# A four-layer transformer kernel: one layer's second residual goes from VectorE to GpSimd, and that layer's loop is written out

## The reference, cut to what matters

```
h   = gamma * norm(x)  + beta
x1  = attention(h) + bp + x              # first residual
out = gamma * norm(x1) + beta + x1       # second residual
```

## Time and profile before

| | |
|---|---|
| median of 3 runs | 1201.8 us (1199.96 to 1210.7) |
| profiled execution | 1202.65 us |
| its span | 1200.8 us |
| TensorE busy in the span | 92% |
| VectorE busy | 67% |
| ScalarE busy | 47% |
| GpSimd busy | 14% |

### The profile page before, as it was taken

The page is one execution under the profiler, slowest core; times in us unless marked ns, Lnnn a source line. Parts: engine busy times, 40 slices in busy tenths (PEclk is TensorE's granted clock), DMA queues, the critical chain, the costliest instruction groups (busy, mean ns, idle before and its releaser), DMA issues.

```text
span 1200.8 us, 22222 instructions
## 1 busy us (share of the span) xinstructions
PE 1100.7 (92%) x7540; PEld 840.9 (70%) x7540; DVE 806.5 (67%) x2245; ACT 560.7 (47%) x1122; POOL 173.5 (14%) x288
## 2 busy tenths in 40 slices
PE   5799999999999999999999988888888999999996
PEld 4567777777777777777777665555555777777765
DVE  4576667666677667766577677777778666776642
ACT  4235554545643455444554434444444455554451
POOL 3010110101102211010110011111114101111010
PEclk9789999999999999999999999999999999999998
DMA  7542333123343233312333323333353133322300
GB/s 234 181 147 72 107 108 92 59 63 105 107 151 147 78 107 107 90 56 70 106 108 116 109 63 115 105 114 112 113 164 124 58 107 116 116 76 65 92 24 18
DMA packets 102714, 123.18 MB, mean 103 GB/s; under 512 B 8992, under 2 KB 96032, under 8 KB 101600
## 3 DMA queue, kind: packets, MB, share of 16 engines
q1 hardware_dynamic: 102048, 121.73, 32.6%
q10 hardware_dynamic: 576, 0.30, 0.1%
HBM read 85.16 MB, written 35.78 MB: 101 GB/s over the span
## 4 chain that ended last, share of the span: by engine, by line
PE 68%; DVE 13%; issue 6%; DMA 5%; ACT 4%; SPq 1%; ACTq 1%; DVEq 0%; POOL 0%; POOLq 0%
PE dense L1160 12%; PE dense L1091 9%; PE s_bank L1184 9%; PE o_bank L1239 8%; PE dense L1146 8%; PE st_bank L1221 6%; DMA q_stack<-max_t 4%; DVE neg_max L790 4%; PE o_bank L1120 3%; PE o_bank L1106 2%; PE o_bank L1070 2%; PE o_bank L1246 2%; PE s_bank L1194 2%; ACT xn L550 2%; DVE s_bank L785 1%
## 5 line engine op out<-in xcount | busy, mean ns | idle before, releaser
L602 ACT ACTIVATE probs<-st_bank 128x512 f32<-128x512 f32 (+1 forms) x512 | 263.8, 568 | 251.8 <-PE st_bank L1221 188.8
L790 DVE TENSOR_REDUCE neg_max<-s_bank 128x2 f32<-128x512 f32 x384 | 256.3, 684 | 70.0 <-PE s_bank L1184 66.1
L1184 PE MATMUL s_bank<-k_stack,q_stack 96*128 96x256 f32 (+1 forms) x1024 | 232.1, 318 | 18.8 <-DMA k_stack<-qk_dram 8.3
L1184 PEld LDWEIGHTS s_bank<-k_stack,q_stack 96*128 96x128 f32 x1024 | 166.1, 194 | 71.1 <-issue 24.5
L1160 PE MATMUL dense<-w_sb,hid 128*128 128x256 f32 x768 | 201.0, 380 | 0.0
L1221 PE MATMUL st_bank<-q_stack,k_stack 98*128 98x512 f32 x384 | 151.2, 467 | 7.7 <-DMA q_stack<-max_t 6.8
L443 POOL TENSOR_TENSOR veps<-mv,eps_c 128x2 f32<-128x2 f32 x65 | 12.7, 195 | 983.6 <-DVE mv L756 902.9
L1239 PE MATMUL o_bank<-probs,v_aug 128*32 128x256 f32 (+1 forms) x2048 | 132.2, 376 | 22.1 <-ACT v_aug L542 18.1
L1160 PEld LDWEIGHTS dense<-w_sb,hid 128*128 128x128 f32 x768 | 130.5, 189 | 10.6 <-issue 0.4
L1091 PE MATMUL dense<-ht,w_sb 128*128 128x256 f32 x512 | 127.4, 389 | 3.8 <-ACT ht L550 1.5
L590 ACT ACTIVATE hid<-dense,vec 128x256 f32<-128x256 f32 x192 | 80.5, 470 | 101.2 <-PE dense L1146 101.2
(11 more groups left out here) (122 smaller groups left out, 1489.9 us busy)
## 6 DMA issues: line engine op xcount, KB each, us to landing
q_stack<-qk_dram SPq DMA_DIRECT2D x192, 128.0 KB, 2.9
k_stack<-qk_dram SPq DMA_DIRECT2D x96, 256.0 KB, 4.1
par_sb<-par_dram SPq DMA_DIRECT2D x32, 512.0 KB, 5.5
qk_dram<-q_hi SPq DMA_DIRECT2D x32, 256.0 KB, 2.2
qk_dram<-q_lo SPq DMA_DIRECT2D x32, 256.0 KB, 2.2
qk_dram<-k_hi SPq DMA_DIRECT2D x32, 256.0 KB, 2.1
qk_dram<-k_lo SPq DMA_DIRECT2D x32, 256.0 KB, 2.1
w_sb<-w SPq DMA_DIRECT2D x3, 1280.0 KB, 9.2
```

The costliest lines, as they stand in the source:

```text
L602: nc.scalar.activation(probs[p % 4][:, kt, :, q0:N], src, ACT.Exp, scale=SCORE_SCALE[l]).then_inc(p_sb, 1)
L790: nc.vector.tensor_reduce(neg_max[:, qt, 2 * p:2 * p + 2], split3(bank[:]), AX.X, ALU.max, negate=True).then_inc(s_max, 1)
L1184: ins = mm(bank[:, e * N:e * N + k1], q_stack[g.par][0:KB, 2 * p + e, qt * P:(qt + 1) * P].bitcast(F32R), k_stack[g.par][0:KB, p, 0:k1].bi ...
```

## The change

Layer 2's second residual leaves VectorE's list and enters GpSimd's, behind `power(n, 0)` and ahead of `addend(g, 0)`: there it is one multiplication and one addition over 128x512 instead of two multiplications over 128x256 and one addition. All eight steps of layer 2 are written out, as layer 1's are. Three waits are new: VectorE's second norm, in every layer, waits for `prod2` of the step before (GpSimd reads `xn2`, which the norm overwrites); the first norm's statistics of layer 3 wait for `x2_done` of the same sequence in layer 2; and the parameter loads of steps 19 to 22, now written out, get SP's wait for `x2_done` that the other written-out steps have.

```diff
@@ run_steps
-                first = B - 1 if CAUSAL[l] else 3
+                written_out = CAUSAL[l] or not HAS_MLP[l]
+                first = B - 1 if written_out else 3
                 for b in range(first):
                     single(Step(l * B + b))
-                if CAUSAL[l]:
+                if written_out:
                     single(Step(l * B + B - 1))
                     continue
@@ sync: step
-                if g.reg is None:
+                if g.reg is None or done.layer == 2:
                     wait(sp, x2_done, done.count(1, 1))
@@ gpsimd
+            def second_residual(c):
+
+                wait(pool, xn2_done, c.count(1, 1))
+                if c.reg is None:
+                    pool.wait_ge(mod_done, modulations_before(c.ahead(1)))
+                nc.gpsimd.tensor_tensor(prod[:], xn2[:], par_sb[c.par][:, 2:3, :].to_broadcast([P, T, D]),
+                                        ALU.mult).then_inc(prod2, 1)
+                wait(pool, prod2, c.count(1, 1))
+                dst = (x_sb[:, bass.ds(c.seq, 1)] if c.reg is not None else x_sb[:, c.seq:c.seq + 1])[:, 0]
+                nc.gpsimd.tensor_tensor(dst, prod[:], xg[1][:], ALU.add).then_inc(x2_done, 1)
@@ gpsimd: step
                 if n.exists:
                     power(n, 0, ln1_mv, ln1_veps, ln1_rstd)
+                    if c.exists and c.layer == 2:
+                        second_residual(c)
@@ vector: ln1_a
+                if i.layer == 3:
+                    wait(dve, x2_done, i.back(B).count(1, 1))
                 norm_stats(x_of(i), 0, ln1_stats)
@@ vector: second_residual
-                if c.layer == 2:
-                    wait(dve, xn2_done, c.count(1, 1))
-                    times_gate(c, xn2, 2, prod2)
-                else:
-                    wait(dve, w2_ps, c.mlp(1, 1))
-                    times_gate(c, split3(dense[1][:]), 2, prod2)
+                wait(dve, w2_ps, c.mlp(1, 1))
+                times_gate(c, split3(dense[1][:]), 2, prod2)
@@ vector: second_norm
+                wait(dve, prod2, c.count(1, 0))
                 if c.layer != 2:
                     wait(dve, w1_ps, c.mlp(4, 0))
@@ vector: step, branch without MLP
                     max_copy(a, 0)
-                    if c.exists:
-                        second_residual(c)
```

## The result

The changed kernel takes 1214.43 us (median of 18 runs, 1210.25 to 1223.95) against 1202.16 us for the kernel before (18 runs); the ratio is 1.0099, 95% interval 1.0076 to 1.0123. It is slower by about 1%, where 1199.2 us and a range of 1197 to 1208 had been forecast. The profiled execution took 1212.57 us.

The account below looks back on a forecast made before the run. VectorE was taken to set the pace in the second half of a layer 2 step. Loop -2.67, ends -0.4, waits +0.4 gave -2.7 us: 1200.0 profiled, 1199.1 on the median, forecast 1199.2 us, range 1197 to 1208.

Parts of the forecast that it names:

- The step that failed: First norm, layer 2: VectorE's second normalization goes ahead of GpSimd's new addition, pair stays 1.46 us, zero charged.
- the second half: Second of VectorE's two first-norm normalizations in layer 2; forecast to run before GpSimd's new addition, at zero cost.
- the first rival: GpSimd's addition runs before VectorE's second normalization: pair 2.50 us, +1.04 us in seven steps, 1206.5 us; chance 0.20.
- the chance of the clock: Rival: TensorE's lower clock spreads to most layer 2 steps, 1.3 us each, 1215.6 us; chance 0.04.
- the hold: GpSimd's addition blocking VectorE's second normalization in layer 2; forecast as a rival, +1.04 us a step, chance 0.20.
- The residual on VectorE is hidden: Layer 2's second residual: its 1.43 us on VectorE are off the path; removing them only adds idle time, zero gain.
- GpSimd's own costs: GpSimd in layer 2: multiplication and addition, 2.6 us per step, hidden; `pick` done at about 739.5; nothing charged.
- the sum for it: GpSimd's list ends at about 739.5, before VectorE's `max_split` at 739.56; zero charged, upper bound 2.1 us.
- The two ends: Steps 17 and 25: work after the residual starts earlier, 0.2 us at each, together -0.4 us.
- The +0.4 us for new waits: VectorE's new waits at seven second norms and three statistics, 0.04 us each.
- The loop: Writing out layer 2's four looped steps: -2.67 us; rival that its cost stays, 1201.3 to 1203 us, chance 0.12.
- The reading of step 24: Straight steps 23 and 24 read as 28.62 and 28.68 us, mean 28.65, used to price writing out the loop.

Follow-up runs that it names:

- the small copy: Changed kernel with one 128x2 GpSimd copy between the residual's multiplication and addition; 1201.18 us, ratio 0.9977.
- the last two versions: Layer 2 written out, GpSimd's addition for the next first residual behind VectorE's first norm; residual early on GpSimd 1198.6 us, on VectorE 1198.83 us.
- the filler: Changed kernel with idle matmuls in TensorE's wait in each layer 2 step; six 1217.45 us, ratio 1.0113; three 1211.56 us, ratio 1.0072.

## Why the prediction was wrong, point by point

**The step that failed.** "The new addition would ask about 0.07 us after, and the second half goes first. I take zero, as before." In the changed kernel the addition starts 0.08 us after the multiplication's end (731.40 + 1.28 = 732.68 to 732.76), as forecast, and it won in each of the eight steps; 0.20 us after it, behind the small copy, it lost in each. What was wrong is the moment at which the first half lets go. The prediction took it from a cast's 0.08 us of stretching. The records of single halves show it directly: step 9 and the end of step 18 before, then the changed kernel, then the small copy's run.

```profile
386.00 1.43 DVE L762 TENSOR_SCALAR xn<-xg,mv,rstd 128x256 f32<-128x256 f32 x1 [0.43 <-POOL rstd L445]
...
735.41 1.13 DVE L762 TENSOR_SCALAR xn<-x_sb,mv,rstd 128x256 f32<-128x256 f32 x1
...
731.73 1.10 DVE L776 TENSOR_SCALAR xn<-x_sb,mv,rstd 128x256 f32<-128x256 f32 x1
732.75 1.43 DVE L776 TENSOR_SCALAR xn<-x_sb,mv,rstd 128x256 f32<-128x256 f32 x1
...
735.70 1.10 DVE L778 TENSOR_SCALAR xn<-x_sb,mv,rstd 128x256 f32<-128x256 f32 x1
736.72 0.40 DVE L778 TENSOR_SCALAR xn<-x_sb,mv,rstd 128x256 f32<-128x256 f32 x1
```

Each time the first half ends 0.15 us after GpSimd's operation: at 387.43 for 387.28, 736.54 for 736.39, 732.83 for 732.68, 736.80 for 736.65. So the cast of step 9 (387.21) came 0.22 us before that end and not 0.08, and an addition 0.08 us behind the multiplication comes 0.07 us before it and not after. The two lines before could be had from the trace of the kernel before, and my margin of 0.07 us was on the wrong side. The small copy moves the addition to 736.85, 0.05 us behind the end of the first half, and then the second half goes first; the copy itself, at 736.71, comes before that end too, but is over at 736.89, and the second half lasts the 0.40 us that it lasted behind the addition at 736.47 before. A trace does not show when an engine asks for a port, so that the end of the first half is the turning point is an inference; all these steps fit it. The price of the first rival, +1.04 us, was right: 1.02 us, pairs of 2.45 to 2.47 us for the forecast 2.50. What can be learned is the weight: a margin of 0.07 us, made of differences of records, does not carry 0.62 against 0.20.

The rule cited from the Trainium skill (SBUF — State Buffer, "Who interferes with whom"), that whoever issues first gets the shared ports for the whole instruction, agrees with the small copy's run, where 0.12 us turned 2.45 into 1.42 us, if the second half's turn is counted from the end of the first. By the starts of the records it does not agree: in the changed kernel the second half's record starts at 732.75 and the addition's at 732.76.

**The second failure: the chance of the clock.** "Step 19 speaks for it, the six other steps at 1.00 against." The six other steps were steps without the hold, so they said nothing on steps with it. The rival was worked out as 1215.6 us and got 0.04; the median is 1214.43. Given the hold it was the likely case, and its price was nearly right as well: 1.17 us a step for the 1.3 taken. That the total came within 1.2 us is in part luck: the base of 1199.2 was low (written out, with the addition behind the pair and with the residual early it is 1199.7 to 1202.7 us), and the two prices were a little high. The range ended at 1208, so the hold alone was inside it and the hold with the clock was not.

**What was right.** The residual on VectorE is hidden: with the addition behind the pair, at full clock, VectorE's idle time behind it is 2.34 us, against 1.10 before and the predicted 1.10 + 1.43 (the 2.58 us above hold some of the lower clock too), and its place made no difference in the last two versions. GpSimd's own costs: 1.28 us for the multiplication, `pick` done at 735.42, well before ScalarE needs it (737.72). `max_split` met nothing; the sum for it comes to 739.6 and not 739.5, so by its own figures it did not quite fit; in the changed kernel it begins at 736.87, 1.4 us behind `pick`, but behind the held pair too. The two ends gained 0.1 and 0.2 us for the 0.2 each: from `max_copy` to the parameter rows of step 17 it takes 707.23 - 705.31 = 1.92 us for the 2.00 before, and the first residual of step 25 comes 0.18 us sooner in the version with the addition behind the pair. The +0.4 us for new waits was not needed: the six steps take 172.42 us with them and 172.47 without.

**The loop.** The steps bear out 2.3 of the 2.67 us, as straight code and at full clock; the whole time of that version is 1.0003 of before, so the gain did not reach the end in full. Its profile shows where a part of it went: step 17 takes 37.45 us (675.41 to 712.86, clock 0.91) where it took 36.06 (676.66 to 712.72, clock 0.95). Whether writing out brings this is not shown; with the addition behind the pair, also written out, step 17 takes 36.3 us. The reading of step 24 in the earlier trace rows was wrong without much effect: 916.16 lies inside TensorE's projection, the next query product starts at 917.99, and step 23 alone would have given 117.27 - 4 x 28.62 = 2.8 us.

**What stays open.** Cut finer, the stretches of the changed kernel show the lower level itself:

```profile
736.88:740.29 3.41, 3.33 (x13) 2.67 (x12) 2.13 (x5) 1.83 (x4) 0.00 (x0) 0.50 0.01 2
...
798.32:805.15 6.83, 6.51 (x20) 4.91 (x19) 2.14 (x5) 2.44 (x6) 0.00 (x0) 0.50 0.02 6
829.04:832.46 3.42, 3.22 (x15) 2.78 (x16) 1.87 (x6) 1.05 (x3) 0.14 (x2) 0.50 0.00 0
```

Step 21 (800.60 to 833.40) is the longest because most of the second and the whole third fall into it; why the second is longer than the others is open. The hold is not the only thing that is followed by the lower level: before, it is there in step 17 (0.50 from 702.35 to 705.77), behind matmuls of 8 columns (698.94 to 702.67), and in step 19 (0.53 from 756.80 to 760.00), behind waits of 1.08 and 0.62 us. That TensorE's wait brings the lower clock is shown by the filler; the filler, however, also adds work, so it shows that a filled gap keeps the clock, and not which property of the gap loses it.

## What to carry to other kernels

An operation moved to GpSimd can be paid for by what VectorE does at that moment: look for VectorE's normalizations from SBUF to SBUF beside it, and put it where VectorE reads PSUM, or behind a semaphore that VectorE raises; both places were free of the hold here. Where two prices depend on the same event, price the case in which they come together, and give it the chance of the event. A margin of less than 0.1 us between two engines, read from differences of records, can fall either way and belongs in the range with both ends. Look for the record that shows the moment itself, here the end of the first half.

## What the runs showed of the hardware that was not expected

A 0.12 us delay of one GpSimd instruction in each of eight steps, made by a copy of 128x2, moved the time of the whole kernel from 1214.4 to 1201.2 us. And 1.5 us of useless matmuls in TensorE's wait shortened six steps of the changed kernel by 1.17 us each, because the granted clock stayed at 1.00 (2.4 GHz) and did not fall to 0.88 to 0.96; in the median of the whole kernel 2.9 us of these 7.0 show.
